# Hadamard matmuls of a staged weight transform: one plain float32 product replaced by two products in the rounded format

## The chip, the cores and the metric

One core of one Trainium2 chip. The metric is the device time of one execution in microseconds (us). One execution has a profile, with the start and length of every instruction on each engine: PE is TensorE (PEld its weight loads), DVE VectorE, ACT ScalarE, POOL GpSimd, SP the queue that issues most DMAs.

## The reference, cut to what matters

```python
def _L0_ffn_ref(x, W1, W2, W3):          # B*S = 4096 tokens, D = 512, H = 2048
    up_gate = jnp.einsum('bsd,hd->bsh', x, W1)
    up_lin = jnp.einsum('bsd,hd->bsh', x, W3)
    hidden = jax.nn.silu(up_gate) * up_lin
    hidden = fwht(hidden)                # Walsh-Hadamard transform over H = 2048, scaled
    out = jnp.einsum('bsh,dh->bsd', hidden, W2)
    return out

x = x + 0.5 * _L0_ffn_ref(_layernorm(x), W1, W2, W3)
x = x + _L0_attn_ref(_layernorm(x), wq, wk, wv, wo, inv_freq)
x = x + 0.5 * _L0_ffn_ref(_layernorm(x), W1, W2, W3)
```

Attention is over the 16 heads of one token, so no token needs another.

## The kernel before, in words

The 4096 tokens are eight tiles of 512. Each tile passes through the feed-forward twice, which makes sixteen passes (numbers 0 to 15). Numbers in float32 are multiplied by splitting each operand into a high part in the rounded format (fp32r) and a low part (the rest, also fp32r) and adding three products, high by high, high by low, low by high. The helper `products` (lines 549 to 553) records these, so lines 551 to 553 are most of TensorE's work. In each pass a loop over n = 0 to 15 handles 128 of the 2048 hidden features per step: `up` makes 24 products of 512 columns into the PSUM tensor gu, ScalarE applies Silu (L875 in pass 0, L917 later), VectorE multiplies by the linear half (L1279 in pass 0), ScalarE and VectorE split the result, and `down` adds it into the PSUM tensor acc.

The Hadamard transform is not applied to the activations but once to W2. That happens in pass 0, beside its `up` steps:

- W2 lies in `tok` as 16 blocks of 128 rows by 512 columns. VectorE does four butterfly stages across the 16 blocks, each stage one subtraction (L1227) and one group of multiply-and-subtract operations (L1234), for three cuts of the columns (168, 168 and 176 wide). The generator `transform` gives out one such piece per `turn`: two before the loop, then two per step n. Its last piece for part 0 (columns 0 to 335) ends in step 6, the last one for part 1 (columns 336 to 511) in step 10; a tiny copy (L1016) then raises `s_fwht`.
- What remains is a 128 by 128 Hadamard matrix within each block. From step 7 on (`HADAMARD_FROM`), right after the `up` of step n, TensorE multiplies four blocks (`BATCH`) by it at L639: plain float32 operands, block as moving operand, `hada` as weights. Steps 7 to 10 do part 0 (336 columns a block), steps 11 to 14 part 1 (176 columns). A batch here is called by its step: batch 7 to batch 14.
- ScalarE scales the results and writes the high part (L880), VectorE the low part (L1288), both into `down_stage`, the room of the attention weights that come later. SP stores it to DRAM for the later passes.

During the same steps ScalarE and VectorE also split the up weights two steps ahead (L861, and `up_low` at L1201). Nothing schedules this at run time: each engine works through its own list in the order written, and waits on semaphores. VectorE's order in a step is: multiply L1279, first turn, `up_low`, the four low parts L1288, second turn. TensorE's `up` of step n waits for `up_low` of n and for the multiply of step n-2; a batch waits for `s_fwht` and for the results of the batch before to be read from PSUM. Pass 0 ends with its `down` products, and all later passes follow.

Of the kernel before, what the change touches and what calls it, by code (L numbers as in the profile page):

```python
# [237 lines left out]
def build(nc, x, up_raw, w2t, attn_raw, inv_freq, hadamard, identity, out):  # L238
    ctx = ExitStack()
    with ctx:  # L240
# [3 lines left out]
        def sem(name):  # L244
            return ctx.enter_context(nc.semaphore(name))
# [41 lines left out]
        s_hada = sem("s_hada")  # L287
        s_freq = sem("s_freq")
# [16 lines left out]
        s_fwht = sem("s_fwht")  # L305
        s_had_ps = sem("s_had_ps")
# [42 lines left out]
        BATCH = 4  # L349
# [19 lines left out]
        def hadamard_batch(n):  # L369

            at = (n - HADAMARD_FROM) * BATCH
            if not 0 <= at < 2 * HT:
                return ()
            return tuple((at // HT, a) for a in range(at % HT, at % HT + BATCH))

# [172 lines left out]
        def _(pe):  # L548
# [73 lines left out]
            def first_pass(X):  # L622

                for n in range(HT):
                    pe.wait_ge(s_up_hi, n + 1)
                    pe.wait_ge(s_up_lo, n + 1)
                    if n >= 2:
                        pe.wait_ge(s_h, n - 1)
                    up(n % 2, X, 0 if n == 0 else None)
                    if n == HADAMARD_FROM:  # L630
                        pe.wait_ge(s_hada, 16)
                    for part, a in hadamard_batch(n):
                        at = HT * part + a
                        if a == 0:
                            pe.wait_ge(s_fwht, part + 1)
                        if at >= BATCH:
                            pe.wait_ge(s_down_hi, at - BATCH + 1)
                            pe.wait_ge(s_down_lo, at - BATCH + 1)
                        nc.tensor.matmul(acc[:, a % BATCH, PARTS[part]], hada[:], tok[:, a, PARTS[part]],  # L639
                                         start=True, stop=True).then_inc(s_had_ps, 1)  # L640
# [187 lines left out]
        def _(act):  # L828
# [38 lines left out]
            for n in range(HT):  # L867
# [14 lines left out]
                if n < SPLIT_FIRST:  # L882
                    act.wait_ge(s_h, n + 1)
                    nc.scalar.activation(hidden_0(n)[0], gated[:, u, :], ACT.Copy).then_inc(s_hid_hi, 1)
            act.wait_ge(s_angle, 1)
# [119 lines left out]
        def _(dve):  # L1005
# [264 lines left out]
            def turn(times):  # L1270

                for _ in range(times):
                    next(w2_turns, None)

            turn(2)
            for n in range(HT):
                u = n % 2
                dve.wait_ge(s_silu, n + 1)
# [15 lines left out]
                turn(1)  # L1294
            angles()
# [211 lines left out]
```

## Time and profile before

| | us |
|---|---|
| three runs, median (lowest to highest) | 2565.17 (2565.13 to 2566.42) |
| the profiled execution, own time | 2565.68 |
| its span, first to last instruction | 2563.9 |
| PE busy in the span | 2531.6 (99%) |
| DVE busy | 2016.7 (79%) |
| ACT busy | 523.0 (20%) |
| mean granted TensorE clock | 0.997 |

A record of a matmul lasts longer than its share of TensorE's time, since matmuls are pipelined; the distance between the starts of two neighbours is what one costs. Engines start and end at times counted from the span's first instruction. "idle before" in a row is the time in which that engine had nothing under way, with the work that ended it.

### The profile page before, as it was taken

To read this page: it belongs to the slowest core of one execution; us is meant where nothing else is said; L and a number is where in the kernel's file an instruction comes from. 1 tells how busy PE (TensorE), PEld (TensorE's weight loads), DVE (VectorE), ACT (ScalarE), POOL (GpSimd) and SP (SyncE) were. 2 spreads that over 40 slices of the span, in tenths; PEclk is the share of its full clock that TensorE was granted. 3 is DMA by queue.
4 is the path that set the end of the run, shared out by engine and by line. 5 is a ranking of instruction groups with operands and counts; after the bars stand their busy time and mean duration, and the time that the engine had idled before them with its cause. 6 is when DMAs were issued, how large, how long until landed. Compare 5 with 4: busy or idle time off the path is not lost.

```text
span 2563.9 us, 30195 instructions
## 1 busy us (share of the span) xinstructions
PE 2531.6 (99%) x11352; PEld 2091.8 (82%) x11352; DVE 2016.7 (79%) x2570; ACT 523.0 (20%) x821; POOL 62.6 (2%) x90
## 2 busy tenths in 40 slices
PE   8999999999999999999999999999999999999999
PEld 7878888888887888888888888888888888888787
DVE  7668979789787897978869889697876979978612
ACT  3312121221121122122212122112121212212111
POOL 0040000000000000000000000000000000000000
PEclk9999999999999999999999999999999999999999
DMA  8654535345452444525525445353552535535354
GB/s 297 241 226 155 189 138 188 117 172 194 156 206 93 164 180 164 213 99 186 189 86 212 147 173 195 116 213 123 197 197 73 189 131 213 189 112 188 117 215 170
DMA packets 91667, 437.46 MB, mean 171 GB/s; under 512 B 8896, under 2 KB 15296, under 8 KB 58304
## 3 DMA queue, kind: packets, MB, share of 16 engines
q1 hardware_dynamic: 84144, 421.70, 44.9%
q10 hardware_dynamic: 7440, 14.68, 1.6%
q8 instruction: 48, 0.79, 0.1%
q14 instruction: 35, 0.29, 0.0%
HBM read 402.79 MB, written 33.55 MB: 170 GB/s over the span
## 4 chain that ended last, share of the span: by engine, by line
PE 94%; DVE 4%; SPq 1%; issue 1%; ACT 0%; DMA 0%; POOLq 0%; DVEq 0%; POOL 0%; ACTq 0%
PE gu L551 20%; PE gu L552 20%; PE gu L553 20%; PE acc L551 10%; PE acc L553 10%; PE acc L552 10%; PE gu L584 1%; PE acc L584 1%; DVE prod L1136 1%; DVE scores L1148 1%; PE acc L639 1%; DVE prod L1141 0%; SPq L481 0%; DVE hid L1299 0%; PE gu L598 0%
## 5 line engine op out<-in xcount | busy, mean ns | idle before, releaser
L551 PE MATMUL gu<-xt,w_up 128*128 128x512 f32 x2048 | 801.1, 391 | 5.8 <-issue 4.6
L553 PE MATMUL gu<-xt,w_up 128*128 128x512 f32 x2048 | 799.0, 390 | 0.0
L552 PE MATMUL gu<-xt,w_up 128*128 128x512 f32 x2048 | 798.9, 390 | 0.0
L551 PEld LDWEIGHTS gu<-xt,w_up 128*128 128x128 f32 x2048 | 385.7, 188 | 86.3 <-issue 6.4
L553 PEld LDWEIGHTS gu<-xt,w_up 128*128 128x128 f32 x2048 | 385.4, 188 | 80.4
L552 PEld LDWEIGHTS gu<-xt,w_up 128*128 128x128 f32 x2048 | 385.6, 188 | 79.9
L1381 DVE TENSOR_TENSOR gated<-gated,gu 128x512 f32<-128x512 f32 x240 | 163.9, 683 | 300.3 <-ACT gated L917 300.0
L917 ACT ACTIVATE gated<-gu 128x512 f32<-128x512 f32 x240 | 143.6, 598 | 1217.6 <-PE gu L553 1217.6
L551 PE MATMUL acc<-w_down,hid 128*128 128x512 f32 x960 | 377.6, 393 | 3.0 <-DVE hid L1388 2.2
L553 PE MATMUL acc<-w_down,hid 128*128 128x512 f32 x960 | 374.1, 390 | 0.0
L552 PE MATMUL acc<-w_down,hid 128*128 128x512 f32 x960 | 374.1, 390 | 0.0
L1136 DVE TENSOR_TENSOR prod<-tok 128x1024 f32<-128x1024 f32 x256 | 309.3, 1219 | 1.0
L1150 DVE TENSOR_REDUCE mixed<-prod 128x64 f32<-128x1024 f32 x256 | 309.8, 1212 | 0.0
L1148 DVE TENSOR_REDUCE scores<-prod 128x32 f32<-128x1024 f32 x256 | 309.3, 1212 | 0.0
L1141 DVE TENSOR_TENSOR prod<-scores,tok 128x1024 f32<-128x1024 f32 x256 | 307.4, 1212 | 1.1
L551 PEld LDWEIGHTS acc<-w_down,hid 128*128 128x128 f32 x960 | 180.3, 188 | 46.1 <-issue 6.8
L925 ACT ACTIVATE hid<-gated 128x512 fp32r<-128x512 f32 x240 | 151.8, 633 | 320.0 <-DVE gated L1381 320.0
L553 PEld LDWEIGHTS acc<-w_down,hid 128*128 128x128 f32 x960 | 180.3, 188 | 37.8
L552 PEld LDWEIGHTS acc<-w_down,hid 128*128 128x128 f32 x960 | 180.4, 188 | 36.0
L1388 DVE TENSOR_TENSOR hid<-gated,hid 128x512 fp32r<-128x512 f32 x240 | 163.9, 683 | 16.2 <-ACT hid L925 15.9
L551 PE MATMUL gu<-w_attn,sub_xt 128*128 128x512 f32 x232 | 91.4, 394 | 7.2 <-DVE sub_xt L1020 4.5
L552 PE MATMUL gu<-w_attn,sub_xt 128*128 128x512 f32 x232 | 90.5, 390 | 0.0
(125 smaller groups left out, 1862.6 us busy)
## 6 DMA issues: line engine op xcount, KB each, us to landing
w_up<-up_pairs SPq DMA_DIRECT2D x240, 1024.0 KB, 4.8
w_down<-down_pairs SPq DMA_DIRECT2D x240, 512.0 KB, 3.4
up_pairs<-w_up SPq DMA_DIRECT2D x16, 1024.0 KB, 4.8
prod<-up_raw SPq DMA_DIRECT2D x16, 512.0 KB, 5.8
down_pairs<-w_attn SPq DMA_DIRECT2D x4, 2048.0 KB, 17.8
out<-x ACTq DMA_DIRECT2D x7, 1024.0 KB, 5.3
x<-x ACTq DMA_DIRECT2D x6, 1024.0 KB, 7.2
tok<-attn_raw SPq DMA_DIRECT2D x4, 1024.0 KB, 18.9
```

What stands on the lines that cost most here:

```text
L551: nc.tensor.matmul(o, w_hi, m_hi, start=first, stop=False)
L552: nc.tensor.matmul(o, w_hi, m_lo, start=False, stop=False)
L553: return nc.tensor.matmul(o, w_lo, m_hi, start=False, stop=last)
L584: ins = nc.tensor.transpose(bank[:, k, s * P:(s + 1) * P], src(s)[:, k * P:(k + 1) * P], ident[:])
L917: nc.scalar.activation(gated[:, u, :], gu[:, 2 * u, :], ACT.Silu).then_inc(s_silu, 1)
L925: nc.scalar.activation(hidden(u)[0], gated[:, u, :], ACT.Copy).then_inc(s_hid_hi, 1)
L1136: return nc.vector.tensor_tensor(prod[:, buf, :].rearrange("p (h t d) -> p h t d", h=2, t=HEADS), wide(q[:, h:h + 2, None, :], 2, HEADS), ...
L1141: return nc.vector.tensor_tensor(prod[:, buf, :].rearrange("p (h d t) -> p h d t", h=2, d=HD), wide(scores[:, g % 2, h:h + 2, None, :], 2, ...
L1148: return nc.vector.tensor_reduce(scores[:, g % 2, h:h + 2, :], prod[:, buf, :].rearrange("p (h t d) -> p h t d", h=2, t=HEADS), AX.X, ALU.add)
L1150: return nc.vector.tensor_reduce(mixed[:, h:h + 2, :], prod[:, buf, :].rearrange("p (h d t) -> p h d t", h=2, d=HD), AX.X, ALU.add)
L1381: nc.vector.tensor_tensor(gated[:, u, :], gated[:, u, :], gu[:, 2 * u + 1, :], ALU.mult).then_inc(s_h, 1)
L1388: nc.vector.tensor_tensor(low, gated[:, u, :], high.bitcast(FP32), ALU.subtract).then_inc(s_hid_lo, 1)
```

## The change

The result of the butterflies is split before TensorE reads it. ScalarE copies the four blocks of the next batch from `tok` to their places in `down_stage` in the rounded format (`high`), VectorE writes the rest beside it (`low`), and TensorE multiplies each block's high and low part by the Hadamard matrix, which has been copied in the rounded format into `sub_xt`, a buffer that is free in pass 0. The entries of the matrix are 1 and -1. Both new operations for batch n+1 stand at the end of step n. In the changed file the split stands at L899 (ScalarE) and L1316 (VectorE), the copy of the matrix at L1295, the two products at L650 and L651.

```diff
+        def mixed_blocks(n):
+            part, a = hadamard_batch(n)[0]
+            cols = PARTS[part]
+            return tok[:, a:a + BATCH, cols], down_stage[:, a:a + BATCH, cols], down_stage[:, a:a + BATCH, D + cols.start:D + cols.stop]
...
                     if n == HADAMARD_FROM:
-                        pe.wait_ge(s_hada, 16)
+                        pe.wait_ge(s_hada_r, 1)
                     for part, a in hadamard_batch(n):
                         at = HT * part + a
-                        if a == 0:
-                            pe.wait_ge(s_fwht, part + 1)
+                        pe.wait_ge(s_mixed_lo, n - HADAMARD_FROM + 1)
                         if at >= BATCH:
                             pe.wait_ge(s_down_hi, at - BATCH + 1)
                             pe.wait_ge(s_down_lo, at - BATCH + 1)
-                        nc.tensor.matmul(acc[:, a % BATCH, PARTS[part]], hada[:], tok[:, a, PARTS[part]],
-                                         start=True, stop=True).then_inc(s_had_ps, 1)
+                        _, high, low = mixed_blocks(n)
+                        o, h = acc[:, a % BATCH, PARTS[part]], sub_xt[:, 0, 0, 0, :]
+                        nc.tensor.matmul(o, h, high[:, a % BATCH], start=True, stop=False)
+                        nc.tensor.matmul(o, h, low[:, a % BATCH], start=False, stop=True).then_inc(s_had_ps, 1)
...
+                if hadamard_batch(n + 1):
+                    act.wait_ge(s_fwht, hadamard_batch(n + 1)[0][0] + 1)
+                    src, high, _ = mixed_blocks(n + 1)
+                    nc.scalar.activation(high, src, ACT.Copy).then_inc(s_mixed_hi, 1)
...
             for n in range(HT):
                 u = n % 2
+                if n == HADAMARD_FROM - 3:
+                    dve.wait_ge(s_hada, 16)
+                    nc.vector.tensor_copy(sub_xt[:, 0, 0, 0, :], hada[:]).then_inc(s_hada_r, 1)
                 dve.wait_ge(s_silu, n + 1)
...
                 turn(1)
+                if hadamard_batch(n + 1):
+                    dve.wait_ge(s_mixed_hi, n + 1 - HADAMARD_FROM + 1)
+                    src, high, low = mixed_blocks(n + 1)
+                    nc.vector.tensor_tensor(low, src, high.bitcast(FP32), ALU.subtract).then_inc(s_mixed_lo, 1)
```

VectorE before, from the last butterfly of part 0 in step 6 to the multiply of step 8 (the copy of `carrier` raises `s_fwht`; x<-gated,gu is the multiply):

```order
L1234 SCALAR_TENSOR_TENSOR tok<-tok 128x8x168
L1016 COPY carrier<-carrier 128x1 [waits s_dve]
L1279 TENSOR_TENSOR x<-gated,gu 128x512 [waits s_silu]
L1227 TENSOR_TENSOR tok<-tok 128x8x176 [waits s_w2_2]
L1201 TENSOR_TENSOR w_up<-prod,w_up 128x1024 [waits s_up_hi,s_dve]
L1288 SCALAR_TENSOR_TENSOR w_attn<-acc,w_attn 128x336 [waits s_down_hi] x4
L1234 SCALAR_TENSOR_TENSOR tok<-tok 128x8x176
L1279 TENSOR_TENSOR x<-gated,gu 128x512 [waits s_silu,s_dve]
```

The same stretch of VectorE now (lines are those of the changed file; w_attn<-tok,w_attn is the new low part, written into `down_stage`, whose tensor is w_attn):

```order
L1249 SCALAR_TENSOR_TENSOR tok<-tok 128x8x168
L1031 COPY carrier<-carrier 128x1 [waits s_dve]
L1316 TENSOR_TENSOR w_attn<-tok,w_attn 128x4x336 [waits s_mixed_hi]
L1297 TENSOR_TENSOR x<-gated,gu 128x512 [waits s_silu]
L1242 TENSOR_TENSOR tok<-tok 128x8x176 [waits s_w2_2]
L1216 TENSOR_TENSOR w_up<-prod,w_up 128x1024 [waits s_up_hi,s_dve]
L1306 SCALAR_TENSOR_TENSOR w_attn<-acc,w_attn 128x336 [waits s_down_hi] x4
L1249 SCALAR_TENSOR_TENSOR tok<-tok 128x8x176
L1316 TENSOR_TENSOR w_attn<-tok,w_attn 128x4x336 [waits s_mixed_hi,s_dve]
L1297 TENSOR_TENSOR x<-gated,gu 128x512 [waits s_silu]
```

One operation over 4 by 336 elements now stands behind the second turn and ahead of the next step's multiply, and it waits for ScalarE.

ScalarE now, from step 6 to the start of step 8 (gated<-gu is Silu, w_attn<-acc the high part of a result; the rows w_attn<-tok are new, the others stood in this order before):

```order
L886 ACTIVATE gated<-gu 128x512 [waits s_h,s_up_done]
L872 ACTIVATE w_up<-prod 128x1024 [waits s_up_stored0,s_up_done,s_up_raw0]
L899 ACTIVATE w_attn<-tok 128x4x336 [waits s_fwht]
L886 ACTIVATE gated<-gu 128x512 [waits s_h,s_up_done]
L872 ACTIVATE w_up<-prod 128x1024 [waits s_up_stored1,s_up_done,s_up_raw1]
L891 ACTIVATE w_attn<-acc 128x336 [waits s_had_ps] x4
L899 ACTIVATE w_attn<-tok 128x4x336 [waits s_fwht]
```

The wait for `s_fwht` moved from TensorE to ScalarE, where the Silu of the next step is queued behind it.

## Rows read from the trace of the kernel before

**Rows 1.** The profile's page: busy time of the engines, and the chain that ended last.
```profile
PE 2531.6 (99%) x11352; PEld 2091.8 (82%) x11352; DVE 2016.7 (79%) x2570; ACT 523.0 (20%) x821; POOL 62.6 (2%) x90
...
PE 94%; DVE 4%; SPq 1%; issue 1%; ACT 0%; DMA 0%; POOLq 0%; DVEq 0%; POOL 0%; ACTq 0%
```
**Rows 2.** Timeline, PE, steps 7 and 11: start, length, engine, line, tiles, [idle before].
```profile
64.08 0.39 PE L553 MATMUL gu<-xt,w_up 128*128 128x512 f32 x1
64.98 2.50 PE L639 MATMUL acc<-tok,hada 128*128 128x336 f32 x8 [0.52 <-DVE carrier L1016]
...
96.11 1.46 PE L639 MATMUL acc<-tok,hada 128*128 128x176 f32 x8
```
**Rows 3.** The chain that ended last, pass 0 and gap: start, length, what.
```profile
88.46 2.26 PE acc L639 x8
...
103.07 1.20 PE acc L639 x8
...
109.72 1.20 PE acc L639 x8
...
191.42 1.75 PE acc L584 x16
```
**Rows 4.** Timeline, DVE, steps 6 to 11.
```profile
59.76 0.69 DVE L1279 TENSOR_TENSOR x<-gated,gu 128x512 f32<-128x512 f32 x1 [0.48 <-ACT gated L875]
...
64.68 0.15 DVE L1016 COPY carrier<-carrier 128x1 f32<-128x1 f32 x1
65.13 0.69 DVE L1279 TENSOR_TENSOR x<-gated,gu 128x512 f32<-128x512 f32 x1 [0.30 <-ACT gated L875]
...
67.39 1.22 DVE L1201 TENSOR_TENSOR w_up<-prod,w_up 128x1024 fp32r<-128x1024 f32 x1
68.53 1.74 DVE L1288 SCALAR_TENSOR_TENSOR w_attn<-acc,w_attn 128x336 fp32r<-128x336 f32 x4
70.20 1.62 DVE L1234 SCALAR_TENSOR_TENSOR tok<-tok 128x1408 f32<-128x1408 f32 x1
73.69 0.69 DVE L1279 TENSOR_TENSOR x<-gated,gu 128x512 f32<-128x512 f32 x1 [1.88 <-ACT gated L875]
...
78.75 1.82 DVE L1234 SCALAR_TENSOR_TENSOR tok<-tok 128x352 f32<-128x352 f32 x4
...
95.91 0.15 DVE L1016 COPY carrier<-carrier 128x1 f32<-128x1 f32 x1
...
103.73 0.69 DVE L1279 TENSOR_TENSOR prod<-gated,gu 128x512 f32<-128x512 f32 x1 [3.69 <-ACT gated L875]
```
**Rows 5.** Groups by shape, 0 to 330 us: count | busy us, mean ns | idle before.
```profile
L861 ACT ACTIVATE w_up<-prod 128x1024 fp32r<-128x1024 f32 x16 | 16.9, 1054 | 14.9 <-DMA prod<-up_raw 14.9
L891 ACT ACTIVATE hid<-x 128x512 fp32r<-128x512 f32 x8 | 5.1, 632 | 19.0 <-PE acc L553 19.0
L1227 DVE TENSOR_TENSOR tok<-tok 128x1344 f32<-128x1344 f32 x8 | 12.4, 1551 | 0.0
L1206 DVE CAST hid<-gated 128x512 fp32r<-128x512 f32 x1 | 0.4, 427 | 0.0
L551 PEld LDWEIGHTS gu<-xt,w_up 128*128 128x128 f32 x256 | 48.8, 190 | 16.5 <-issue 6.4
L639 PEld LDWEIGHTS acc<-tok,hada 128*128 128x128 f32 x64 | 11.0, 190 | 4.0 <-issue 0.9 <-DVE carrier L1016 0.3
```
**Rows 6.** Timeline, PE: two places where TensorE had stood idle.
```profile
28.89 0.76 PE L551 MATMUL gu<-xt,w_up 128*128 128x512 f32 x1 [4.58 <-issue]
29.45 0.63 PE L552 MATMUL gu<-xt,w_up 128*128 128x512 f32 x1
...
831.37 0.51 PE L551 MATMUL gu<-w_attn,sub_xt 128*128 128x512 f32 x1 [2.71 <-DVE tok L1119]
```
**Rows 7.** Windows: us, busy of each engine, granted clock (PEclk), DMA share, GB/s.
```profile
28.00:32.00 4.00, 3.11 (x7) 2.48 (x8) 3.96 (x8) 1.70 (x3) 0.00 (x0) 0.50 0.88 312
828.00:832.00 4.00, 1.29 (x6) 0.72 (x6) 3.18 (x7) 0.60 (x1) 0.00 (x0) 1.00 0.02 4
```

More of the change, by code:

```diff
@@ L287, in build @@
         s_hada = sem("s_hada")
+        s_hada_r = sem("s_hada_r")
         s_freq = sem("s_freq")
@@ L305, in build @@
         s_fwht = sem("s_fwht")
+        s_mixed_hi = sem("s_mixed_hi")
+        s_mixed_lo = sem("s_mixed_lo")
         s_had_ps = sem("s_had_ps")
```

## The prediction

> **What bounds the kernel now.** I read the page first: TensorE is busy 99% of the span, and the chain that ended last is 94% TensorE and 4% VectorE [rows 1]. So a microsecond taken from TensorE's list counts, if nobody else is late, and so does every microsecond that it waits. Then TensorE's timeline where the change sits, then VectorE's beside it. Batch 7 already waits: TensorE's last `up` product starts at 64.08, the batch at 64.98, released by VectorE's marker copy behind the butterflies [rows 2]. VectorE is nearly full in these steps. Before the multiply of step 6 it had 0.48 us to spare, in step 7 it works from 65.13 to 71.82 (70.20 + 1.62) without a gap and then has 1.88 us, in step 8 from 73.69 to 80.57 [rows 4]. From step 11 on it has plenty, 3.69 us before the multiply of step 12 [rows 4]. So in steps 6 to 10 two engines are almost equally loaded, in steps 11 to 14 only TensorE is.
>
> **TensorE's side.** A batch of part 0 costs 2.26 us now (8 records, two a block), one of part 1 1.20 us; the `up` between two batches is 109.72 - 103.07 - 1.20 = 5.45 us for 24 products, 0.227 us each at 512 columns [rows 3]. 512 columns at 2.4 GHz are 0.213 us, so a rounded product costs its columns once and some 0.014 us more. The new batch has 8 such products. At 336 columns that gives 0.140 + 0.014 = 0.154 us each, 1.23 us a batch: 1.03 us less than now, in four batches. At 176 columns it would give 0.087 us, but no product of this trace comes so quickly: the narrowest ones, 16 of 128 columns, took 1.75 us, 0.110 us each, where their columns are 0.053 us [rows 3]. From below the price is 0.087, from above 0.150, what each of the eight plain records of the same width takes (1.20 / 8). I take the 0.110 of the narrow row: 0.88 us a batch, 0.32 us less than now, in four batches. TensorE's list so becomes 4 x 1.03 + 4 x 0.32 = 5.4 us shorter.
>
> The 0.110 rests on the weight load. Rounded weights load in 190 ns a record, plain ones in 190 ns too [rows 5]. The Trainium skill, "TensorE: Matmul & The Clock Gate", section on Fast Weight Load, has a quick load for 128 weights of any type but FP32. Were the rounded format such a type, the narrow product would cost its columns, and the sum below would be 3.1 us instead of 3.8; the two equal rows speak against that.
>
> **VectorE's and ScalarE's side.** Prices: ScalarE takes 632 ns for 512 elements and 1054 ns for 1024 [rows 5], 0.824 ns an element, so the high copy takes 1.32 us for 4 x 336 elements and 0.79 us for 4 x 176. VectorE takes 1551 ns for two inputs of 1344 elements [rows 5], exactly the size of the new low part, and 0.69 us for 512 [rows 4], so 0.89 us for 704. The matrix's copy is at most 0.43 us (512 elements took 427 ns [rows 5], it has 128; about 0.2). It comes in step 4, and the 0.48 us before step 6 covers it; I cost it at nothing (without that cover it would be 0.2).
>
> The first batch. `s_fwht` comes at 64.83 as before (64.68 + 0.15) [rows 4]. ScalarE, which now waits for it, copies from 64.87 to 66.19; VectorE's low part runs from 66.22 to 67.77, and batch 7 starts 0.15 us later (as from 64.83 to 64.98 [rows 2, 4]), at 67.92. Now it is 64.98: **2.9 us lost**. The Silu and multiply of step 7 are queued behind the two new operations; the multiply starts at about 67.7 instead of 65.13.
>
> Steps 7 to 9. From there VectorE is the later one. Its own work in a step is 6.69 us (step 7) or 6.88 us (step 8, four small pieces in the turn) [rows 4]; steps 9 and 10 I take as 6.7. To this comes the low part, 1.55 us, less 0.08 us by which a following operation overlaps (67.39 + 1.22 against 68.53 [rows 4]) plus 0.03 for the wait on its source. So low parts end at 67.77, 75.96 (+8.19), 84.34 (+8.38) and 92.54 (+8.20). TensorE would need 5.45 + 1.23 = 6.7 us a step, so it is ready earlier and its saving in batches 7 to 10 **buys nothing**. ScalarE does not bind: its results of a batch are out before VectorE reaches L1288.
>
> Step 10. VectorE's work ends with the marker at 92.46 + 6.7 + 0.19 = 99.35, the high copy at 100.17, the low part at 101.09, batch 11 starts at 101.24. Now it starts at 96.11 [rows 2]: **5.1 us behind**.
>
> Steps 11 to 14. TensorE's period is 5.45 + 0.88 = 6.33 us. VectorE has the multiply, `up_low`, four results of 176 columns and the low part of 0.89, under 5 us, so it is ready first (batch 12: low part by 104.8, TensorE at 107.6). TensorE gains 4 x 0.32 = 1.3 us back.
>
> Sum: 5.1 - 1.3 = **3.8 us slower**. Behind batch 14 nothing changes its order; `down`, the stores and the attention weights all start from this point and shift with it. The profiled execution would go from 2565.68 to 2569.5, the median from 2565.17 to 2569.0. The profiled execution lies 0.5 us above the median, inside the runs shown. About 0.2% (5.1 us) is what a measurement of this kernel can tell from no change, so this counts as "within", close to its edge.
>
> **Bounds of this case.** With the narrow product at 0.087 us the sum is 3.1 us, at 0.150 us it is 5.1. The wide product does not matter up to (8.19 - 5.45) / 8 = 0.34 us. The case's own range is 2568.2 to 2570.3.
>
> **Rivals.**
> 1. *Narrow rounded products run at the plain rate.* A block of 176 columns costs 2 x 0.150 = 0.30 us as one plain product. All rounded products of the trace have 512 columns; if at 176 columns one of them costs as much as a plain one, a block costs 0.60 us and a batch 2.40. That adds 1.20 us in four batches: 5.1 + 4.8 = 9.9 us, 2575.1. It decides against "within" from 0.16 us a product on. For it: the narrow row costs twice its columns. Against it: that row is explained by a load time as well, and nothing shows two rates.
> 2. *The clock falls in the wait before batch 7.* TensorE would have nothing under way from 64.47 to 67.92, 3.4 us. After 4.58 us idle the clock stood at 0.50 and products came 0.43 us apart; after 2.71 us it stayed at 1.00 [rows 6, 7]. 3.4 lies between. At the 1.2 GHz level for some 5 us, as after the row with 4.58, batch 7 and the first third of step 8's `up` cost 2.4 us more, of which 0.4 to 1.1 us is covered by TensorE's slack before batch 8: some 2.0 us, 5.8 in all, 2571.0. It would show as products 0.43 us apart right behind the wait. The Trainium skill ("TensorE: Matmul & The Clock Gate", "What's actually happening") also has idleness bring the half rate back; rows 6 and 7 agree.
> 3. *Faster: the split hides.* If VectorE's additions fitted beside TensorE, the 5.4 us of TensorE's list would come out in full, 2559.8. The place is the low part at the end of steps 6 to 9. In the two steps whose work rows 4 show, TensorE would need 6.7 us and VectorE without it 6.7 to 6.9, so there is no room for it at all unless two inputs of this shape cost far less than 1551 ns; it decides from a low part of some 0.3 us down. For it speaks only that VectorE still shows 1.88 us idle ahead of step 8 [rows 4], which TensorE's own savings would take away. Rows 5 speak against it.
> 4. *The rounded products are no such thing* (the blocks run as plain ones at all widths): 4.5 us a part-0 batch, period 9.97, batch 11 at 107.8, then 4.8 more, in all 16.5 us, 2581.7. The 0.227 us of every `up` product speaks against it.
>
> **How the numbers follow.** The forecast gets 0.57, rival 1 0.25, rival 2 0.10, rival 3 0.05, rival 4 0.03. Predicted 2569.0. The range takes in the forecast from some 1 us below its lower end, rivals 2 and 1: 2567.2 to 2575.5. Out of the forecast 0.09 lies beyond +5.1 us (narrow products near 0.150, or VectorE slower than counted), and 0.02 of rival 2 below. Slower: 0.09 + 0.25 + 0.07 + 0.03 = 0.44. Faster: 0.04, most of rival 3. Within: 0.52.
>
> **What would show it.** In the changed profile batch 7 starts near 67.9 with over 3 us of idle TensorE ahead of it, released by VectorE's low part; batches 8 to 11 start near 76.1, 84.5, 92.7 and 101.2, each released by the low part; batches 12 to 14 follow without a wait, 6.3 us apart. Low parts last 1.55 and 0.89 us. Eight products of 336 columns take 1.2 us, eight of 176 columns 0.9 (rival 1: 2.4). I am wrong if VectorE keeps gaps in steps 7 to 10, if batch 11 starts more than 1 us from 101.2, or if the difference grows or shrinks behind batch 14.

## The result, and the profile after

| | before | after |
|---|---|---|
| median of the runs | 2565.97 us (2565.13 to 2569.27, 20 runs) | 2570.24 us (2567.87 to 2577.53, 20 runs) |
| profiled execution | 2565.68 us, span 2563.9 | 2569.62 us, span 2567.8 |
| ratio of the medians | | 1.0017, 95% interval 1.0010 to 1.0024 |

The changed kernel is 4.3 us slower, 0.17%: just inside the bound of "no change", as forecast (2569.0 us), and the interval excludes a gain. The ratios of this document leave out three executions at a low clock, far above the others of their kernel: 2816.33 us without the low part, 2669.41 and 4867.69 us with the new waits filled. The profile's page for it, busy times and chain:

```profile
PE 2527.3 (98%) x11352; PEld 2089.3 (81%) x11352; DVE 2025.9 (79%) x2579; ACT 531.1 (21%) x829; POOL 62.8 (2%) x90
...
PE 94%; DVE 4%; SPq 1%; issue 0%; ACT 0%; DMA 0%; POOLq 0%; DVEq 0%; POOL 0%; ACTq 0%
```

Against [rows 1] TensorE is 4.3 us less busy and VectorE 9.2 us more, and the span is 3.9 us longer: TensorE got shorter work and longer waits. Where the waits are can be read in TensorE's timeline of the changed kernel (start, length, engine, line, tiles, in brackets the idle time before and who ended it):

```profile
67.41 0.47 PE L650 MATMUL acc<-w_attn,sub_xt 128*128 128x336 f32 x1 [3.46 <-DVE w_attn L1316]
67.67 0.48 PE L651 MATMUL acc<-w_attn,sub_xt 128*128 128x336 f32 x1
67.95 0.48 PE L650 MATMUL acc<-w_attn,sub_xt 128*128 128x336 f32 x1
...
75.75 0.31 PE L650 MATMUL acc<-w_attn,sub_xt 128*128 128x336 f32 x1
75.90 0.32 PE L651 MATMUL acc<-w_attn,sub_xt 128*128 128x336 f32 x1
...
85.11 0.65 PE L650 MATMUL acc<-w_attn,sub_xt 128*128 128x336 f32 x1 [2.50 <-DVE w_attn L1316]
...
102.72 0.35 PE L650 MATMUL acc<-w_attn,sub_xt 128*128 128x176 f32 x1 [2.40 <-DVE w_attn L1316]
102.91 0.28 PE L651 MATMUL acc<-w_attn,sub_xt 128*128 128x176 f32 x1
103.02 0.27 PE L650 MATMUL acc<-w_attn,sub_xt 128*128 128x176 f32 x1
103.13 0.28 PE L651 MATMUL acc<-w_attn,sub_xt 128*128 128x176 f32 x1
```

Batch 7 waits 3.46 us for VectorE's low part (L1316) and starts at 67.41 instead of 64.98 [rows 2]. Batch 11 starts at 102.72 instead of 96.11. A wide rounded product follows the one before after 0.15 us (75.75, 75.90), a narrow one after 0.11 (102.91, 103.02, 103.13). But behind the first wait the wide ones are 0.26 to 0.28 us apart, which fits rival 2 and no other case of the forecast. The windows of the same trace tell why (stretch, its length, busy time of PE, PEld, DVE, ACT and POOL, granted clock, DMA share, GB/s):

```profile
64.00:68.00 4.00, 0.59 (x3) 0.62 (x4) 2.58 (x5) 2.75 (x3) 0.00 (x0) 0.95 0.97 309
68.00:72.00 4.00, 4.00 (x15) 3.54 (x15) 3.97 (x6) 3.02 (x5) 0.00 (x0) 0.63 0.90 348
...
84.00:88.00 4.00, 2.89 (x10) 2.80 (x11) 3.97 (x4) 1.79 (x5) 0.00 (x0) 0.58 0.34 133
```

The granted clock fell to its 1.2 GHz level behind the wait before batch 7 and again behind the one before batch 9; in the kernel before all windows from 64 to 88 us stand at 1.00. VectorE's timeline shows what that did to the other side:

```profile
59.24 0.69 DVE L1297 TENSOR_TENSOR x<-gated,gu 128x512 f32<-128x512 f32 x1 [0.48 <-ACT gated L886]
...
65.70 1.56 DVE L1316 TENSOR_TENSOR w_attn<-tok,w_attn 128x1344 fp32r<-128x1344 f32 x1 [1.39 <-ACT w_attn L899]
67.18 0.68 DVE L1297 TENSOR_TENSOR x<-gated,gu 128x512 f32<-128x512 f32 x1
...
73.88 1.56 DVE L1316 TENSOR_TENSOR w_attn<-tok,w_attn 128x1344 fp32r<-128x1344 f32 x1
76.58 0.69 DVE L1297 TENSOR_TENSOR x<-gated,gu 128x512 f32<-128x512 f32 x1 [1.14 <-ACT gated L886]
...
94.06 0.69 DVE L1297 TENSOR_TENSOR x<-gated,gu 128x512 f32<-128x512 f32 x1 [0.76 <-ACT gated L886]
```

The low part takes 1.56 us and is the last thing in its step, as counted. But VectorE, which I had without a gap from 67.8 to 101, waits 1.14 us and 0.76 us for the Silu of an `up` that TensorE finished late.

**A fixed mark.** The start of the program differs by up to 1.9 us between profiled executions (the multiply of step 6 starts at 58.24 to 60.11 us). So from here I count each trace from that multiply, 59.76 in the kernel before [rows 4], and compare the starts of batch 11 and of the last `up` of pass 0. Behind a plain batch this `up` is counted from the batch's start plus its 1.20 us, because the record of its first product starts 0.13 us sooner; the start of pass 0's `down`, which needs no such rule, gives the same differences within 0.05 us:

| from the multiply of step 6 | batch 7 | batch 11 | last `up` of pass 0 | median, ratio to before (95%) |
|---|---|---|---|---|
| before | 5.22 | 36.35 | 57.65 | |
| the change | 8.17 | 43.48 (+7.13) | 63.53 (+5.88) | 2570.24, 1.0017 (1.0010 to 1.0024) |
| forecast for it | 8.16 | +5.1 | +3.8 | 2569.0 |

The loss in pass 0 was 2.0 us larger than forecast. In this profiled execution part of it came back at the very end. TensorE waits 5.31 us before the last pass and then makes sixteen transposes of 128 columns (L584, L594 in the changed file); from their start to the end of the program it takes 137.5 us (2430.30 to 2567.8), before 139.05 (2424.85 to 2563.9). From the mark to the end the change is 4.42 us behind.

```profile
2430.30 3.27 PE L594 MATMUL acc<-ident,tok 128*128 128x128 f32 x16 [5.31 <-DVE tok L1067]
2433.32 0.48 PE L561 MATMUL gu<-xt,w_up 128*128 128x512 f32 x1
2433.64 0.40 PE L562 MATMUL gu<-xt,w_up 128*128 128x512 f32 x1
```

### The profile page after: what moved, and what is told of

Its sections match the earlier page's. It is cut to its first block, busy times and chain, and to the rows that moved or that the text cites. A ratio compares the mean times of both kernels' runs of the same rounds, so it can differ in the third digit from the quotient of the medians.

```text
span 2567.8 us, 30212 instructions
## 1 busy us (share of the span) xinstructions
PE 2527.3 (98%) x11352; PEld 2089.3 (81%) x11352; DVE 2025.9 (79%) x2579; ACT 531.1 (21%) x829; POOL 62.8 (2%) x90
## 4 chain that ended last, share of the span: by engine, by line
PE 94%; DVE 4%; SPq 1%; issue 0%; ACT 0%; DMA 0%; POOLq 0%; DVEq 0%; POOL 0%; ACTq 0%
PE gu L561 20%; PE gu L562 20%; PE gu L563 20%; PE acc L561 10%; PE acc L562 10%; PE acc L563 10%; PE gu L594 1%; PE acc L594 1%; DVE prod L1151 1%; DVE scores L1163 1%; SPq L491 0%; DVE hid L1321 0%; PE gu L608 0%; DMA prod<-up_raw 0%; DVE prod L1156 0%
```

## The experiments

My theory after the result: VectorE's additions set batches 7 to 11, as forecast (+3.8 at the mark), and a fall of the granted clock in the new waits adds some 2 us. Rivals: rounded products dearer than counted at the batch (rival 1), and the copy or the dependency chain, not VectorE's low part, being what costs. The experiments ran in three groups, each with runs of the kernel before on the same chip, to which its ratios refer: median 2565.79 us for the first four, 2566.55 for the next four, 2565.92 for the last three.

### Without the low part

```diff
-                        pe.wait_ge(s_mixed_lo, n - HADAMARD_FROM + 1)
+                        pe.wait_ge(s_mixed_hi, n - HADAMARD_FROM + 1)
...
-                        nc.tensor.matmul(o, h, low[:, a % BATCH], start=False, stop=True).then_inc(s_had_ps, 1)
+                        nc.tensor.matmul(o, h, high[:, a % BATCH], start=False, stop=True).then_inc(s_had_ps, 1)
...
-                if hadamard_batch(n + 1):
-                    dve.wait_ge(s_mixed_hi, n + 1 - HADAMARD_FROM + 1)
-                    src, high, low = mixed_blocks(n + 1)
-                    nc.vector.tensor_tensor(low, src, high.bitcast(FP32), ALU.subtract).then_inc(s_mixed_lo, 1)
```

> The changed kernel without VectorE's low part of the blocks: TensorE waits for ScalarE's high copy and multiplies that twice, so what the low part adds to the result is left out, and the number of products stays. If VectorE's low part is what holds batches 8 to 11 back, VectorE's step falls from 8.2 to 6.7 us, batch 7 starts about 1.3 us later than in the kernel before (one copy of 1.32 us and its handover), batch 11 about 1 us earlier, the narrow products give 1.3 us more, and the time is some 2.4 us below the kernel before (2563 to 2564 if that has 2566). If the handover to ScalarE or the falling clock is what costs, batch 11 stays 3 us or more behind and the time stays above the kernel before.

Measured: 2566.24 us, ratio 1.0002 (0.9992 to 1.0011). At the mark batch 7 is at 6.58, batch 11 at 35.69 (0.66 ahead of before) and the last `up` at 57.31 (0.34 ahead). So the copy and the longer chain of handovers are not what costs: without VectorE's low parts, five of which stand ahead of batch 11, the whole loss in pass 0 is gone. Batch 11 comes 7.8 us earlier than in the change; this includes the falls of the clock, which did not occur before batch 11 here, where the wait before batch 7 is 1.87 us and not 3.46. The time I had expected, 2563 to 2564, was missed. TensorE's timeline and the windows of this run show two falls of the clock:

```profile
95.80 0.52 PE L650 MATMUL acc<-w_attn,sub_xt 128*128 128x176 f32 x1 [2.08 <-ACT w_attn L899]
96.11 0.42 PE L651 MATMUL acc<-w_attn,sub_xt 128*128 128x176 f32 x1
```
```profile
96.00:100.00 4.00, 4.00 (x16) 3.54 (x17) 2.91 (x6) 2.79 (x7) 0.00 (x0) 0.60 0.46 188
832.00:836.00 4.00, 4.00 (x12) 3.19 (x13) 0.00 (x0) 0.00 (x0) 0.00 (x0) 0.63 0.00 0
```

The clock fell in a wait of 2.08 us, and from batch 11 to batch 12 it takes 8.04 us instead of the change's 6.46. It fell once more behind the wait of 2.71 us at 831 us, where it had stayed at 1.00 before [rows 6, 7]; that cost 1.6 us.

### Without any splitting

```diff
-                        pe.wait_ge(s_mixed_lo, n - HADAMARD_FROM + 1)
+                        if a == 0:
+                            pe.wait_ge(s_fwht, part + 1)
...
-                        nc.tensor.matmul(o, h, high[:, a % BATCH], start=True, stop=False)
-                        nc.tensor.matmul(o, h, low[:, a % BATCH], start=False, stop=True).then_inc(s_had_ps, 1)
+                        nc.tensor.matmul(o, h, hid[:, 0, 0, PARTS[part]], start=True, stop=False)
+                        nc.tensor.matmul(o, h, hid[:, 0, 0, PARTS[part]], start=False, stop=True).then_inc(s_had_ps, 1)
```
ScalarE's high copies and VectorE's low parts are taken out too.

> The changed kernel without both parts of the split: TensorE waits for the butterflies as before and multiplies zeros of the same shapes in the rounded format, so the Hadamard products are left out of the result, not their time. If the products themselves save what the forecast counted (1.03 us a wide batch, 0.32 us a narrow one), TensorE and VectorE are level in steps 7 to 10 at 6.7 to 6.9 us, batch 11 starts about 3.5 us earlier than in the kernel before and the time is 4.8 us below it. If rounded products are dearer than that, the time is less than 2 us below the kernel before.

Measured: 2561.99 us, ratio 0.9987 (0.9978 to 0.9996); batch 7 at 5.22 as before, batch 11 2.84 us ahead (3.5 expected), the last `up` 4.08 ahead; the median is 3.8 below the kernel before (4.8 expected). The clock fell here too behind the wait of 2.71 us (window from 828 to 832 us: 0.57), for 1.6 us, so the time holds less of the gain than it could. So of the 5.4 us that TensorE's list got shorter (rival 3's sum) even a splitting at no cost gives back 4.1 us; VectorE's old work takes the rest, as the bracket before batch 11 shows, which still ends with VectorE's marker:

```profile
92.51 0.35 PE L651 MATMUL acc<-hid,sub_xt 128*128 128x176 f32 x1 [1.25 <-DVE carrier L1028]
```

### The splitting with plain products

```diff
-                        nc.tensor.matmul(o, h, high[:, a % BATCH], start=True, stop=False)
-                        nc.tensor.matmul(o, h, low[:, a % BATCH], start=False, stop=True).then_inc(s_had_ps, 1)
+                        nc.tensor.matmul(acc[:, a % BATCH, PARTS[part]], hada[:], tok[:, a, PARTS[part]],
+                                         start=True, stop=True).then_inc(s_had_ps, 1)
```

> The changed kernel with both parts of the split and their waits, but with one plain float32 product a block as before: it tells what the split costs alone. If VectorE sets batches 7 to 10, the wide products' saving was worth nothing: batch 11 starts where the changed kernel has it or up to 1 us earlier (a longer batch leaves less idle time for the clock to fall), only the 1.3 us of the narrow batches are missing, and the time is 1.3 us or less above the changed kernel, some 4.5 to 5.5 us above the kernel before. If TensorE's saving in part 0 did count, it is 5.4 us above the changed kernel.

Measured: 2574.77 us, ratio 1.0034 (1.0021 to 1.0048), 4.5 us above the change and 9.0 above the kernel before, both more than expected (at most 1.3, and 4.5 to 5.5). Batch 11 is at +8.01, 0.9 later than in the change, where I had it the same or earlier. So the forecast's "the wide saving buys nothing" does not hold where the clock falls. Here batch 7 ran behind the same wait at the low clock, and as plain products it took 4.19 us; VectorE then waited 1.97 us, not 1.14:

```profile
67.18 4.19 PE L650 MATMUL acc<-tok,hada 128*128 128x336 f32 x8 [3.46 <-DVE w_attn L1316]
```
```profile
77.50 0.69 DVE L1297 TENSOR_TENSOR x<-gated,gu 128x512 f32<-128x512 f32 x1 [1.97 <-ACT gated L886]
```

From batch 11 to the last `up` it loses nothing more and gains nothing (+8.01 and +8.01), while the change gains 1.25 us there: this is the 1.3 us of the narrow products. The rest lies behind pass 0: a further fall of the clock at 148.8 us, where one stretch takes 15.01 us and 13.38 in the change, and the last stretch behind the 5.31 us wait, 138.99 us against 137.5. In these two executions that makes 0.9 + 1.3 + 1.6 + 1.5 = 5.3 us from the mark to the end. It is close to the 5.4 us that I had named as the sign that TensorE's saving counts in full, but only 2.1 us of it arise in pass 0.

### The new waits filled with products

TensorE makes products of 512 columns on zeros, which nobody reads, in the waits before batches 7 to 11, so that it is never long idle there. The output is the change's.

```diff
+        FILL = {7: 13, 8: 4, 9: 5, 10: 5, 11: 8}
...
+                    if n in FILL:
+                        pe.wait_ge(s_h, n)
+                        for _ in range(FILL[n]):
+                            nc.tensor.matmul(gu[:, 2 * ((n + 1) % 2), :], hid[:, 0, 0, 0:P], hid[:, 0, 0, :], start=True, stop=True)
```

> The changed kernel with products on zeros, 13, 4, 5, 5 and 8 of them, written to a PSUM bank that the next up overwrites, in TensorE's waits before batches 7 to 11. Nothing else differs. If the falling clock took the 1.14 and 0.76 us for which VectorE waited for Silu in steps 8 and 10, the granted clock stays at 1.00 from 40 to 120 us, VectorE has no idle time there, batch 11 starts about 5.1 us later than in the kernel before, the spread between runs narrows and the median is some 1.5 us below the changed kernel's. If the clock is not what separates the runs, the time is that of the changed kernel within 0.5 us, or above it.

Measured at the mark: batch 7 at 8.08, batch 11 at 41.51 (+5.16), the last `up` at 61.46 (+3.81). The forecast had 5.1 and 3.8. The clock stays at 1.00 from 33 to 120 us:

```profile
64.00:68.00 4.00, 3.57 (x19) 2.87 (x18) 3.30 (x3) 3.17 (x7) 0.00 (x0) 1.00 0.96 290
84.00:88.00 4.00, 4.00 (x20) 3.35 (x19) 3.97 (x7) 2.18 (x4) 0.00 (x0) 1.00 0.26 102
144.00:148.00 4.00, 4.00 (x11) 3.14 (x12) 0.44 (x1) 0.00 (x0) 0.00 (x0) 0.57 1.00 414
```

The low parts of this run start 8.18, 8.39 and 8.25 us apart, where the forecast has 8.19, 8.38 and 8.20, and VectorE waits for nothing between them and through step 10:

```profile
64.70 1.56 DVE L1321 TENSOR_TENSOR w_attn<-tok,w_attn 128x1344 fp32r<-128x1344 f32 x1 [1.39 <-ACT w_attn L904]
...
72.88 1.56 DVE L1321 TENSOR_TENSOR w_attn<-tok,w_attn 128x1344 fp32r<-128x1344 f32 x1
...
81.27 1.56 DVE L1321 TENSOR_TENSOR w_attn<-tok,w_attn 128x1344 fp32r<-128x1344 f32 x1
...
89.52 1.56 DVE L1321 TENSOR_TENSOR w_attn<-tok,w_attn 128x1344 fp32r<-128x1344 f32 x1
```

So the two parts of the loss are told apart: 3.8 us is VectorE's chain, the further 2.07 us at the mark (5.88 - 3.81) is the clock in the new waits. But the median was 2570.64, ratio 1.0019 (1.0009 to 1.0029), where I had expected 1.5 us or more below the change: the window from 144 to 148 us shows a fall that had not been there, behind a wait of 1.97 us which the kernel before has as well. There products came 0.43 us apart:

```profile
143.89 0.58 PE L562 MATMUL acc<-w_attn,hid 128*128 128x512 f32 x1 [1.97 <-DVE hid L1326]
144.27 0.63 PE L563 MATMUL acc<-w_attn,hid 128*128 128x512 f32 x1
144.70 0.63 PE L564 MATMUL acc<-w_attn,hid 128*128 128x512 f32 x1
```

From there to the next such wait it takes 15.02 us, before 13.43. The last stretch, 138.97 us against the change's 137.5, took back another 1.5 us. So what was won by batch 11 was lost again later, and filling only the new waits made the program no faster.

### Only the last three batches split

```diff
+        ROUNDED = (12, 13, 14)
...
-                if hadamard_batch(n + 1):
+                if n + 1 in ROUNDED:
...
+                        if n in ROUNDED:
...
+                        else:
+                            nc.tensor.matmul(acc[:, a % BATCH, PARTS[part]], hada[:], tok[:, a, PARTS[part]],
+                                             start=True, stop=True).then_inc(s_had_ps, 1)
```

> The kernel before with the change made for batches 12 to 14 alone, where VectorE waited 3.5 us in every step; batches 7 to 11 keep one plain product a block, and the rounded copy of the matrix moves to step 11. If the rest of the theory holds (products of 176 columns at 0.110 us, split hidden), each of the three batches takes 0.88 instead of 1.20 us, nobody waits, and TensorE's last up of pass 0 starts 1.0 us earlier than in the kernel before: 1.0 us faster, which the timing may or may not resolve. If the handover costs something there too, the three batches start later and it is no faster or slower.

Measured: 2564.40 us, ratio 0.9992 (0.9983 to 1.0001), so by the runs' times alone a gain is not settled. Batch 11 is at 36.37, 0.02 from before, the last `up` 0.95 us ahead: three times the forecast's 0.32. VectorE keeps its idle time while it does the three low parts, so the same kind of operation (here of 704 elements, not 1344) that cost 5.1 us in the steps before costs nothing here:

```profile
98.96 0.88 DVE L1325 TENSOR_TENSOR w_attn<-tok,w_attn 128x704 fp32r<-128x704 f32 x1
...
102.69 0.69 DVE L1306 TENSOR_TENSOR prod<-gated,gu 128x512 f32<-128x512 f32 x1 [2.86 <-ACT gated L895]
```

### Three low parts on GpSimd

```diff
+        BY_POOL = (8, 9, 10)
...
+            for n in BY_POOL:
+                pool.wait_ge(s_mixed_hi, n - HADAMARD_FROM + 1)
+                src, high, low = mixed_blocks(n)
+                nc.gpsimd.tensor_tensor(low, src, high.bitcast(FP32), ALU.subtract).then_inc(s_mixed_pl, 1)
...
-                if hadamard_batch(n + 1):
+                if hadamard_batch(n + 1) and n + 1 not in BY_POOL:
```

> The changed kernel with the low parts of batches 8, 9 and 10 made by GpSimd, which is idle in these steps, and those of batches 7 and 11 to 14 by VectorE. If VectorE's 1.5 us a step are all that holds the batches back, its step falls to 6.7 to 6.9 us, batch 11 starts about 0.7 us later than in the kernel before and the narrow batches give 1.3 us more: 0.6 us faster than the kernel before at the same clock. If GpSimd and VectorE get in each other's way (in pass 0 of the kernel before a VectorE operation of 0.68 us took 1.84 us beside GpSimd's work on the attention weights), VectorE's operations beside it grow and the batches come as late as in the changed kernel or later.

Measured: 2576.70 us, ratio 1.0032 (1.0020 to 1.0044); batch 11 at +7.59, the last `up` at +8.99, worse than with VectorE doing it. The two timelines of this run, GpSimd's and VectorE's:

```profile
71.90 3.10 POOL L1008 TENSOR_TENSOR w_attn<-tok,w_attn 128x1344 fp32r<-128x1344 f32 x1 [63.70 <-ACT w_attn L904]
87.40 3.27 POOL L1008 TENSOR_TENSOR w_attn<-tok,w_attn 128x1344 fp32r<-128x1344 f32 x1 [3.63 <-ACT w_attn L904]
```
```profile
72.76 3.73 DVE L1258 SCALAR_TENSOR_TENSOR tok<-tok 128x1408 f32<-128x1408 f32 x1
87.75 4.00 DVE L1225 TENSOR_TENSOR w_up<-prod,w_up 128x1024 fp32r<-128x1024 f32 x1
```

VectorE's operations beside the GpSimd one take 3.73 us instead of 1.62, and 4.00 instead of 1.22 [rows 4]. Both end about one usual length after the GpSimd operation has ended (76.49 against 75.00 + 1.62, 91.75 against 90.67 + 1.22), as if they had waited for it. Beside the GpSimd operation for batch 9 the four small pieces of step 8 take 3.19 us instead of 1.82 [rows 4]. So VectorE's list loses three low parts, 4.50 us, and gets 6.26 us back in stretched neighbours.

From these rows batch 11 can be estimated: 5.16 us (the change at full clock) - 4.50 + 6.26 + 0.73 us, for which VectorE waits for the Silu of step 8 behind the fall of the clock at 68 us, is +7.65, and +7.59 was measured. The step to +8.99 is the clock: it fell behind the wait of 4.14 us before batch 11, and from there to batch 12 it takes 9.12 us instead of 6.46. A third fall, at 164 us, stands behind an old wait of 1.97 us.

### The same change once more

One look at the unchanged kernel, to see whether the falls of the clock are chance.

> The changed kernel once more, for its clock alone. If the falls of the clock in waits of 2 to 3.5 us come and go from one execution to the next, they are at other places here than in the first profile (there behind the waits before batches 7 and 9), the waits themselves are the same, and the time follows: about 0.9 to 1.4 us less where one of them is missing. If they belong to the program, they are at the same places.

Measured: 2570.33 us; batches 7 and 11 are at 8.16 and 43.46, the last `up` at 63.51, all within 0.02 us of the first trace. The two falls are at the same places, so as far as two traces tell they belong to the program:

```profile
68.00:72.00 4.00, 3.86 (x13) 3.56 (x14) 3.97 (x5) 2.73 (x5) 0.00 (x0) 0.57 0.94 362
84.00:88.00 4.00, 2.17 (x8) 2.18 (x9) 3.93 (x5) 1.90 (x4) 0.00 (x0) 0.67 0.52 174
```

The shorter last stretch is there again too, 137.59 us from the transposes (2430.91) to the end (2568.5):

```profile
2430.91 3.32 PE L594 MATMUL acc<-ident,tok 128*128 128x128 f32 x16 [5.31 <-DVE tok L1067]
```

### Three batches split, and the gap before the last pass filled

The version above, and 21 products for nobody in the wait of 5.31 us near the end, behind which the clock had fallen in every trace so far.

```diff
+                if p == NP - 1:
+                    pe.wait_ge(s_added, SUBS * p)
+                    for _ in range(21):
+                        nc.tensor.matmul(acc[:, 0, :], w_attn[:, O, 0, 0, 0:P], w_attn[:, O, 0, 0, :], start=True, stop=True)
```

> The kernel with the change for batches 12 to 14 alone, and 21 products without use into a free PSUM bank in the wait of 5.31 us before the transposes of the last pass. If the clock falls in that wait in every execution and costs what the profile before shows (16 transposes in 3.3 instead of 1.75 us, and some 6 products at 0.43 instead of 0.23 us), the stretch from the first transpose to the end shrinks from 139.05 to about 136.3 us, and the time is 3.5 to 4 us below the kernel before. If the fall costs nothing because something else bounds the last pass, it is 1 us below.

Measured: 2562.79 us, ratio 0.9987 (0.9978 to 0.9996). TensorE's timeline there, first of the kernel before, then of this one:

```profile
2424.85 3.68 PE L584 MATMUL acc<-ident,tok 128*128 128x128 f32 x16 [5.31 <-DVE tok L1052]
2428.18 0.78 PE L551 MATMUL gu<-xt,w_up 128*128 128x512 f32 x1
```
```profile
2423.63 1.97 PE L595 MATMUL acc<-ident,tok 128*128 128x128 f32 x16 [0.55 <-DVE tok L1080]
2425.80 0.47 PE L562 MATMUL gu<-xt,w_up 128*128 128x512 f32 x1 [0.20 <-DVE xt L1048]
```

The sixteen transposes take 1.97 us and not 3.68, and from their start to the end of the program it is 136.67 us instead of 139.05 (and 139.06 in the three-batch version without the filling): 2.4 us for products that compute nothing. In the medians the two three-batch versions are 1.6 us apart, and this one is 3.8 us below its kernel before, as expected.

### All kernels with the waits filled

To compare the change at equal clock, each of three kernels got that filling, seven products in each of the two waits of 1.97 us (near 142 and 155 us in the kernel before) and nine in the one of 2.71 us: the kernel before; the change with the waits before batches 7 to 11 filled as well; the three-batch version.

```diff
+                    if n in (6, 10):
+                        pe.wait_ge(s_h, HT)
+                        for _ in range(7):
+                            nc.tensor.matmul(gu[:, 0, :], xt[0][:, 0, 0, 0:P], xt[0][:, 0, 0, :], start=True, stop=True)
...
+                    if p == 5:
+                        for _ in range(9):
+                            nc.tensor.matmul(acc[:, 3, :], w_attn[:, O, 0, 0, 0:P], w_attn[:, O, 0, 0, :], start=True, stop=True)
```

> The kernel before with products without use in four of TensorE's waits behind pass 0's up steps: 7 in each of the two waits of 1.97 us in pass 0's down, 9 in the wait of 2.71 us at 831 us, 21 in the wait of 5.31 us before the last pass. If the runs of one kernel differ mainly by where the clock falls, the only fall left is the one at 28 us, the time is some 2.5 us below the kernel before (median 2563.5) and the runs lie within 2 us of each other. If they differ by something else, the spread stays at 4 to 5 us.

> The changed kernel with the same four fills and those of the waits before batches 7 to 11. With no fall of the clock but the one at 28 us in either, the difference to the kernel before with the four fills is what the change costs by its waits alone: 3.8 us if VectorE's chain is all of it. If the filled kernels differ by clearly more, the change has a cost outside the stretch that was counted; if by less than 2.5 us, part of the 3.8 is won back later.

> The kernel with the change for batches 12 to 14 alone and the four fills. It should be 1.0 us faster than the kernel before with the same fills, and the fastest of all correct ones here, about 2562.5 us. If the 1.0 us does not last to the end, it is level with the kernel before with the fills.

| filled | batch 11 | last `up` of pass 0 | median (range, 11 runs) | ratio to before (95%) |
|---|---|---|---|---|
| the kernel before | 36.35 | 57.62 | 2563.50 (2562.66 to 2564.00) | 0.9989 (0.9980 to 0.9998) |
| the change | 41.50 | 61.47 | 2567.07 (2565.89 to 2567.74) | 1.0002 (0.9993 to 1.0011) |
| three batches | 36.37 | 56.71 | 2563.03 (2561.66 to 2563.98) | 0.9987 (0.9978 to 0.9996) |

In the change's trace the places where the clock had fallen in one kernel or another now read:

```profile
64.00:68.00 4.00, 3.57 (x18) 2.80 (x17) 2.73 (x3) 3.17 (x5) 0.00 (x0) 1.00 0.97 305
144.00:148.00 4.00, 3.59 (x16) 2.88 (x16) 1.05 (x2) 0.35 (x1) 0.00 (x0) 1.00 1.03 423
2428.00:2432.00 4.00, 3.81 (x25) 3.25 (x24) 2.48 (x4) 2.07 (x4) 0.00 (x0) 1.00 0.00 0
```

With no fall left but the one at 28 us, which all kernels have [rows 7], the change costs 2567.07 - 2563.50 = **3.6 us**, and 3.85 us at the mark. That is the forecast's sum of 3.8 to within 0.2 us. The three-batch version is 0.5 us below the filled kernel before in the medians, where 1.0 was expected; their ranges overlap, so in the runs' times that gain isn't settled. The traces show 0.91 us of it at the end of pass 0, and 0.65 from the mark to the end of the program. The expectations for the kernel before with the fills, 2563.5 us and runs within 2 us of each other, came out.

The fastest versions are thus the two with three batches split and waits filled, 2562.79 and 2563.03 us, 2.9 to 3.8 us or some 0.13% under the kernel before and 7 us under the change. By the filled kernel before, 2.4 us of it is the filling, not the rounded products.

## Why the prediction was right or wrong

**VectorE's and ScalarE's prices** held: low parts 1.56 and 0.89 us (1.55 and 0.89), high copy 1.32 (1.32), batch 7 at 8.17 from the multiply (8.16).

**TensorE's prices** held: 0.11 us for the narrow product, 0.15 for the wide one. The 0.110 was taken from a row of transposes (L584), which are not rounded products; that both cost the same could not be known from it. That transposes of 128 columns and products of 176 cost the same 0.110 us speaks against a price by columns. The loads of the changed kernel fit a bound by the weights:

```profile
102.83 0.19 PEld L651 LDWEIGHTS acc<-w_attn,sub_xt 128*128 128x128 f32 x1
102.94 0.19 PEld L650 LDWEIGHTS acc<-w_attn,sub_xt 128*128 128x128 f32 x1
```

They start 0.11 us apart, while 176 columns at 2.4 GHz are 0.073. No run varies the load alone, so the weights as the bound stay argued. The prediction's other case, in which the rounded format loads quickly and the sum is 3.1, is out: the loads last as long as plain ones. The Trainium skill ("TensorE: Matmul & The Clock Gate", "Weight-path perf modes — Fast Weight Load (FWL) and DoubleRow") has the quick load for every type but FP32; here the rounded format did not get it. Rival 1 (2575.1) and rival 4 (2581.7) fall with the same rows.

**Steps 7 to 10** held as a mechanism: with the clock at 1.00 batch 11 was 5.16 and 5.15 us behind (5.1). In the change itself, of batches 8 to 11, only 9 and 11 wait for their low part, where I had named all four; to 8 and 10 TensorE came late on its own, through the falls of the clock. "Its saving in batches 7 to 10 buys nothing" is shown by no run at full clock, though the sum that contains it came out; at the low clock the saving was worth 0.9 us at batch 11, as the run with plain products showed. Rival 3 (2559.8) fell: without the low parts the loss is gone, with them the split hides nowhere in steps 6 to 9.

**Steps 11 to 14** held: 1.25 us back in the change, 1.35 and 1.30 in its two filled versions, 1.3 forecast.

**What failed is the weight of rival 2.** I gave the fall of the clock in the 3.4 us wait 0.10, between a wait of 4.58 us with a fall and one of 2.71 without. The trace of the kernel before had a second fall that I did not weigh, behind the 5.31 us wait near its end (granted clock 0.50 from 2424 to 2428 us). Behind the wait before batch 7 it fell in all four traces that have 3.46 us there (the change twice, plain products, GpSimd), and it was not even the only place: behind the 2.50 us before batch 9 it fell in both traces of the change, where the forecast has only 1.7 us of slack (8.38 - 6.7) and says nothing of the clock. That wait grew because VectorE had lost 1.14 us while TensorE was slow. The 2.71 us that I took as the length at which the clock stays was one row taken for a rule: behind the same wait it fell in three other traces. The price for rival 2, 2.0 us, agrees with the 2.07 measured at the mark, but for another sum: two falls, through which VectorE waited 1.14 and 0.76 us. (A slip beside it: I counted 0.07 of rival 2 as slower, though 0.10 less the 0.02 below is 0.08; nothing hangs on it.)

**What made the median come near anyway.** The change is 5.88 us behind at the end of pass 0 and 4.3 in the medians. In the profiled executions some 1.5 us came back because after the last wait the clock was down for less time (139.05 us to the end before, 137.50 and 137.59 in the two traces of the change, where the products behind the transposes are 0.23 us apart from the second on, while before the first ones came 0.43 apart). So that the median came within 1.3 us of 2569.0 is in part luck: the forecast rests on a mechanism that was right to 0.1 us and on two errors about the clock that partly cancel, falls in the new waits that it did not count, and a shorter fall at the end that it did not count either. Why the last part was shorter stays open. The change does not decide it alone: the nine traces in which this wait is not filled fall into two kinds, four with 138.97 to 139.06 us (the kernel before, three batches, plain products, the new waits filled) and five with 137.50 to 138.05 (the change twice, GpSimd, no low part, no splitting). Among the change's 20 runs the time goes with the run's mean clock, 2567.87 to 2568.54 us at 0.998 and 2572.38 to 2572.84 at 0.995, which fits falls that come and go from run to run; the traces cannot show it, since only the change was traced twice, with its falls at the same places.

**The signs that I had named.** Batch 11 is more than 1 us from its forecast (43.48 at the mark, forecast 36.35 + 5.1 = 41.45), the difference shrank behind batch 14, and VectorE has gaps before the multiplies of steps 8 and 10. By its own test the forecast is wrong in the clock and right in the chain.

## What to carry to other kernels

Splitting operands so that TensorE runs cheaper products moves work to VectorE and ScalarE, and its worth is decided stage by stage: here the same kind of operation cost 5.1 us in the five steps where VectorE was full, and nothing a few steps later, where VectorE stood idle. Before adding a wait of 2 us or more on a busy TensorE, read the granted clock behind every wait of the trace, and give a fall a price and a chance. A few products for nobody in the wait keep the clock, and filling all waits can be worth more (2.4 us here) than three rounded batches; filling only the new ones gained nothing in the median. When two edits are compared, compare them from a fixed mark, since the start of the program moved by 1.9 us and single falls of the clock by 1.6 us, both larger than the 1 us that three batches give.

## What the runs showed of the hardware that I had not expected

- **The clock falls behind short waits, but not behind all.** It fell behind 3.46 us (4 of 4 traces), 2.50 (2 of 2), 2.08 (1 of 1), 4.14 (1 of 1), and 3 of 20 times behind the two waits of some 1.97 us that ten traces have; it stayed at 1.00 behind 2.40 us in both traces of the change, and behind the wait of 2.7 us near 830 us in seven traces while it fell behind that same wait in three. So the length of a wait alone doesn't tell. A fall that stood alone behind 1.97, 2.08 or 2.71 us cost 1.5 to 1.6 us, in seven places; the one behind 5.31 us cost from 0.8 us (137.50 against 136.67) to 2.4 us. The Trainium skill ("TensorE: Matmul & The Clock Gate", "What's actually happening") has idleness bring the half rate back; the traces agree, and here the clock fell behind waits as short as 1.97 us.
- **Filling the old waits made the time steadier.** The runs of the kernel before spread over 4.8 us (2564.86 to 2569.69, 27 runs), those of the same kernel with the fills over 1.3 us, of the other two filled kernels over 1.9 and 2.3 us (11 runs each). With the last wait alone filled the three-batch version still spread over 4.8 us (11 runs).
- **A GpSimd operation of 3.1 us more than doubled its neighbours on VectorE,** 1.62 to 3.73 us and 1.22 to 4.00, though the engines wrote different tiles. One of the two neighbours read other columns of the tile that GpSimd read, the other worked on other tiles altogether.
